# Route stage of a fused transformer kernel: two buffers for divided and residual rows, the division three trips ahead, the logits one trip later, the residual addition on GpSimd

## The reference, cut to what matters

```
ctx = einsum('bhst,bthd->bshd', attn, v).reshape(B, S, d)   # second attention, 16 heads of 16
X = X + ctx @ wo
h2 = rmsnorm(X, norm2_w).reshape(B * S, d)                  # x * rsqrt(mean(x*x) + 1e-6) * w
logits = h2 @ router_w                                      # 256 x 8
...                                                         # top 2 of 8 experts, weights
return X + moe_out                                          # and the outer: h = h + ffn(layernorm(h))
```

## Time and profile before

| | us |
|---|---|
| three runs | 825.42, 825.05, 827.81 (median 825.42) |
| the profiled execution | 832.71 |
| span of the profiled execution, first to last instruction | 830.6 |
| TensorE busy in it | 754.3 (91%) |
| VectorE busy | 465.3 (56%) |
| ScalarE busy | 376.0 (45%) |
| GpSimd busy | 189.5 (23%) |

### The profile page before, as it was taken

The page is one execution under the profiler, slowest core; times in us unless marked ns, Lnnn a source line. Parts: engine busy times, 40 slices in busy tenths (PEclk is TensorE's granted clock), DMA queues, the critical chain, the costliest instruction groups (busy, mean ns, idle before and its releaser), DMA issues. The chain is left out here.

```text
span 830.6 us, 19023 instructions
## 1 busy us (share of the span) xinstructions
PE 754.3 (91%) x7136; PEld 565.8 (68%) x7137; DVE 465.3 (56%) x1111; ACT 376.0 (45%) x616; POOL 189.5 (23%) x294
## 2 busy tenths in 40 slices
PE   4799999999988995899997888999899999999993
PEld 2366776667667884355554764555599999999992
DVE  7677666667536652799983783721244444444441
ACT  4677777777633443167764232201233333333330
POOL 5500000000003343233230220045412222222222
PEclk9999999999979999599999887999999999999997
DMA  5300000000011345344464900012423323332321
GB/s 176 146 2 2 2 3 2 2 2 2 3 46 39 102 129 168 97 125 125 115 226 144 356 1 16 0 60 79 158 63 51 47 49 45 51 50 46 45 45 19
DMA packets 70543, 58.95 MB, mean 71 GB/s; under 512 B 7552, under 2 KB 62152, under 8 KB 70480
## 3 DMA queue, kind: packets, MB, share of 16 engines
q1 hardware_dynamic: 62048, 47.61, 18.6%
q0 software_dynamic: 7152, 9.38, 6.9%
q10 hardware_dynamic: 1280, 1.08, 0.4%
HBM read 35.02 MB, written 22.95 MB: 70 GB/s over the span
## 5 line engine op out<-in xcount | busy, mean ns | idle before, releaser
L1443 POOL DMA_INDIRECT out<-ex_Y,ex_to x39 | 60.6, 1553 | 167.8 <-DVE ex_Y L1709 160.6
L1192 DVE TENSOR_REDUCE fa_m<-ps 128x2 bf16<-128x512 f32 x128 | 85.0, 685 | 8.9 <-PE ps L1063 7.3
L1162 ACT ACTIVATE fa_PT<-ps 128x1024 f32<-128x1024 f32 x64 | 65.4, 1025 | 47.7 <-PE ps L1078 45.5
L1667 DVE TENSOR_TENSOR ex_hT<-ps,ex_sl 128x512 f32<-128x512 f32 x39 | 27.0, 692 | 102.6 <-PE ps L1509 102.6
L640 ACT ACTIVATE la_PT<-ps 128x512 f32<-128x512 f32 x128 | 69.5, 594 | 25.9 <-PE ps L545 25.5
L1509 PEld LDWEIGHTS ps<-ex_xT,V 128*128 128x128 f32 x640 | 76.2, 195 | 1.7 <-ACT ex_xT L1562 0.7
L1509 PE MATMUL ps<-ex_xT,V 128*128 128x128 f32 x640 | 76.4, 279 | 0.5 <-ACT ex_xT L1562 0.5
L1516 PE MATMUL ps<-WD,ex_hT 128*128 x312 | 73.9, 380 | 0.8 <-DVE ex_Y L1709 0.8
L1509 PEld LDWEIGHTS ps<-ex_xT,XS 128*128 128x128 f32 x608 | 70.8, 192 | 1.6 <-ACT ex_xT L1562 0.7
L1509 PE MATMUL ps<-ex_xT,XS 128*128 128x128 f32 x608 | 71.1, 275 | 0.5 <-ACT ex_xT L1562 0.5
L1063 PE MATMUL ps<-QK 96*128 96x256 bf16 x256 | 53.6, 297 | 10.9 <-PEq L766 8.9
(11 more groups left out here) (260 smaller groups left out, 1430.9 us busy)
## 6 DMA issues: line engine op xcount, KB each, us to landing
QK<-qk_parts SPq DMA_DIRECT2D x192, 64.0 KB, 2.3
qk_parts<-pj_parts SPq DMA_DIRECT2D x16, 384.0 KB, 2.7
expert_in<-zfill SPq DMA_DIRECT2D x1, 5070.0 KB, 16.0
ex_XR<-expert_in SPq DMA_DIRECT2D x39, 130.0 KB, 2.1
WG<-in_e_gate SPq DMA_DIRECT2D x8, 512.0 KB, 7.8
WU<-in_e_up SPq DMA_DIRECT2D x8, 512.0 KB, 10.0
WD<-in_e_down SPq DMA_DIRECT2D x8, 512.0 KB, 9.3
out<-HS SPq DMA_DIRECT2D x4, 512.0 KB, 4.6
```

What stands on the lines that cost most here:

```text
L1162: nc.scalar.activation(PT[:, y % 2, 2 * (x % 2):2 * (x % 2) + 2], ps[:, 2 + 2 * (x % 2):4 + 2 * (x % 2)].rearrange("p k (j i) -> p k j i", ...
L1192: nc.vector.reduce_max(m[:, b % 2, grp, 2 * k:2 * k + 2], ps[:, h % 2].rearrange("p (f j) -> p f j", f=2), AX.X).then_inc(s_max, 1)
L1443: nc.gpsimd.indirect_dma_start(out=outs, out_offset=bass.IndirectOffsetOnAxis(ap=to[:, n:n + 1], axis=0), in_=Y[:, n], in_offset=None, com ...
```

## The change

- `AT` and `X2` get two buffers each, used in turn by pair.
- TensorE's trip t becomes: rows t+3, logits t-1, output t+1, divided rows t+2, normalized rows t. The last logits follow the last trip.
- VectorE's trip t becomes: X2 and moments t+1, division t+3, normalization t+1, logits copy t. Ahead of the trips stand division 0, division 1, moments 0, division 2, normalization 0.
- The addition to `HS` goes from VectorE to GpSimd, which does it as soon as X2 is there, ahead of its power (semaphore `residual`; X2 of pair i waits for the addition of pair i-2).
- ScalarE copies the turned normalized rows straight to `H2T`, from which the logits are formed; the tile `hT` and the second copy go. ScalarE now copies `ATT` of t+2 ahead of the normalized rows of t.
- The increment of `s_apart` behind bn_stats goes, and the loops of VectorE, ScalarE and GpSimd are written out.
- The banks `ps[:, 0:2]` of the rows, the bank of the output and the waits on them stay as they are.

```diff
--- before.py
+++ after.py
@@ -732,12 +732,12 @@
                             s.rec[:].unsqueeze(2).to_broadcast([P, GT * H, DK]), ALU.mult).then_inc(s.at, 1)
 
 
-def head_buffers(g, c, nc, tag):
+def head_buffers(g, c, nc, tag, n=1):
 
     def sb(n, sh):
         return c.enter_context(nc.sbuf_tensor(tag + n, sh, F32))
     s = Shared()
-    s.AT, s.ATT, s.rec = sb("AT", [P, GT, D]), sb("ATT", [P, DC, GC]), sb("rec", [P, GT * H])
+    s.AT, s.ATT, s.rec = sb("AT", [P, GT, D] if n == 1 else [P, n, GT, D]), sb("ATT", [P, DC, GC]), sb("rec", [P, GT * H])
     s.rows, s.recip, s.at, s.att, s.attc = (g.sem(tag + n) for n in ("rows", "recip", "at", "att", "attc"))
     return s
 
@@ -1204,14 +1204,15 @@
 
 
     sem, ps = g.sem, g.ps
-    (s_in, s_h, s_x2, s_var, s_r2, s_hn, s_ht, s_htc, s_h2, s_lg, s_lgk, s_dv, s_half, s_kept, s_apart) = (
-        sem("rt_" + n) for n in "in h x2 var r2 hn ht htc h2 logits lkept dve half kept apart".split())
+    (s_in, s_h, s_x2, s_var, s_r2, s_hn, s_ht, s_htc, s_lg, s_lgk, s_dv, s_half, s_kept, s_res) = (
+        sem("rt_" + n) for n in "in h x2 var r2 hn ht htc logits lkept dve half kept residual".split())
     with ExitStack() as c:
         def sb(n, sh, dt):
             return c.enter_context(nc.sbuf_tensor("rt_" + n, sh, dt))
-        s = head_buffers(g, c, nc, "rt_")
+        s = head_buffers(g, c, nc, "rt_", 2)
         st, mv, half = sb("st", [P, GT, 6], F32), sb("mv", [P, GT, 6], F32), sb("half", [P, GT], F32)
-        X2, hn, hT = sb("X2", [P, GT, D], F32), sb("hn", [P, GT, D], F32), sb("hT", [P, DC, GC], F32)
+        X2 = sb("X2", [P, 2, GT, D], F32)
+        hn = sb("hn", [P, GT, D], F32)
         w2, W, rw = sb("w2", [P, D], F32), sb("W", [P, DC, D], F32), sb("rw", [P, DC, E], F32)
         with nc.Block() as block:
             @block.sync
@@ -1228,16 +1229,27 @@
             def _(pool):
                 nc.gpsimd.memset(half[:], -0.5).then_inc(s_half, 1)
                 pool.wait_ge(s_half, 1)
-                with pool.Fori(0, GN) as t:
+                for t in range(GN):
+                    at = slice(t * GT, (t + 1) * GT)
+                    pool.wait_ge(s_x2, t + 1)
+                    nc.gpsimd.tensor_tensor(g.HS[:, at], g.HS[:, at], X2[:, t % 2], ALU.add).then_inc(s_res, 1)
                     pool.wait_ge(s_var, t + 1)
                     nc.gpsimd.tensor_tensor(mv[:, :, 4], mv[:, :, 3], half[:], ALU.pow).then_inc(s_r2, 1)
-
                     pool.wait_ge(s_hn, t * GT + GT)
-                    nc.gpsimd.tensor_copy(g.XS[:, bass.ds(t * GT, GT), 0:D], hn[:]).then_inc(s_kept, 1)
+                    nc.gpsimd.tensor_copy(g.XS[:, at, 0:D], hn[:]).then_inc(s_kept, 1)
 
             @block.tensor
             def _(pe):
                 mm = nc.tensor.matmul
+
+                def turn_att(i):
+                    pe.wait_ge(s.at, i + 1)
+                    if i:
+                        pe.wait_ge(s.attc, i)
+                    for k in range(GT):
+                        for c in range(DC):
+                            last = nc.tensor.transpose(ps[:, 2, c * GC + k * P:c * GC + (k + 1) * P], s.AT[:, i % 2, k, c * P:(c + 1) * P], g.identF[:])
+                    last.then_inc(s.att, 1)
 
                 def output(i):
                     pe.wait_ge(s.attc, i + 1)
@@ -1260,47 +1272,40 @@
                     pe.wait_ge(s_lgk, i + 1)
                     for k in range(GT):
                         for cc in range(DC):
-                            last = mm(ps[:, 5, k * E:(k + 1) * E], hT[:, cc, k * P:(k + 1) * P], rw[:, cc], start=cc == 0, stop=cc == DC - 1)
+                            last = mm(ps[:, 5, k * E:(k + 1) * E], g.H2T[:, cc, i * GC + k * P:i * GC + (k + 1) * P], rw[:, cc], start=cc == 0, stop=cc == DC - 1)
                     last.then_inc(s_lg, 1)
 
-                for i in range(2):
-                    pe_turn_rows(nc, pe, g, s, i)
-                    if i == 1:
-                        pe.wait_ge(s_in, 48)
-                        output(0)
-                    pe_turn_att(nc, pe, g, s, i)
-
-                def trip(t, ahead):
-                    if ahead:
-                        pe_turn_rows(nc, pe, g, s, t + 2)
-                    output(t + 1)
+                pe_turn_rows(nc, pe, g, s, 0)
+                pe_turn_rows(nc, pe, g, s, 1)
+                turn_att(0)
+                pe_turn_rows(nc, pe, g, s, 2)
+                pe.wait_ge(s_in, 48)
+                output(0)
+                turn_att(1)
+                for t in range(GN):
+                    if t + 3 < GN:
+                        pe_turn_rows(nc, pe, g, s, t + 3)
+                    if t:
+                        logits(t - 1)
+                    if t + 1 < GN:
+                        output(t + 1)
+                    if t + 2 < GN:
+                        turn_att(t + 2)
                     turn_normed(t)
-                    if ahead:
-                        pe_turn_att(nc, pe, g, s, t + 2)
-                    logits(t)
-
-                for t in range(GN - 2):
-                    trip(t, True)
-                trip(GN - 2, False)
-                turn_normed(GN - 1)
                 logits(GN - 1)
 
             @block.scalar
             def _(act):
                 def turned(i):
                     act.wait_ge(s_ht, i + 1)
-                    nc.scalar.activation(hT[:], ps[:, 4].rearrange("p (c t) -> p c t", c=DC), ACT.Copy).then_inc(s_htc, 1)
-                    act.wait_ge(s_htc, i + 1)
-                    nc.scalar.activation(g.H2T[:, :, bass.ds(i * GC, GC)], hT[:], ACT.Copy).then_inc(s_h2, 1)
-                    act.wait_ge(s_h2, i + 1)
-
-                for i in range(2):
-                    act_keep_att(nc, act, g, s, i, s_h)
-                with act.Fori(0, GN - 2) as t:
+                    nc.scalar.activation(g.H2T[:, :, i * GC:(i + 1) * GC], ps[:, 4].rearrange("p (c t) -> p c t", c=DC), ACT.Copy).then_inc(s_htc, 1)
+
+                act_keep_att(nc, act, g, s, 0, s_h)
+                act_keep_att(nc, act, g, s, 1, s_h)
+                for t in range(GN):
+                    if t + 2 < GN:
+                        act_keep_att(nc, act, g, s, t + 2, s_h)
                     turned(t)
-                    act_keep_att(nc, act, g, s, t + 2, s_h)
-                for i in range(GN - 2, GN):
-                    turned(i)
 
             @block.vector
             def _(dve):
@@ -1311,15 +1316,16 @@
                     dve.wait_ge(s_h, i + 1)
                     if not first(i):
                         dve.wait_ge(s_hn, i * GT)
-                    V.tensor_tensor(X2[:], ps[:, 3].rearrange("p (k d) -> p k d", d=D), g.XS[:, bass.ds(i * GT, GT), 0:D], ALU.add).then_inc(s_x2, 1)
+                    if i >= 2:
+                        dve.wait_ge(s_res, i - 1)
+                    V.tensor_tensor(X2[:, i % 2], ps[:, 3].rearrange("p (k d) -> p k d", d=D), g.XS[:, bass.ds(i * GT, GT), 0:D], ALU.add).then_inc(s_x2, 1)
                     dve.wait_ge(s_x2, i + 1)
                     for k in range(GT):
-                        do(V.bn_stats(st[:, k], X2[:, k]), s_apart)
+                        do(V.bn_stats(st[:, k], X2[:, i % 2, k]))
                         do(V.bn_aggr(mv[:, k, 0:2], st[:, k]))
                     do(V.tensor_tensor(mv[:, :, 2], mv[:, :, 0], mv[:, :, 0], ALU.mult))
                     do(V.tensor_tensor(mv[:, :, 2], mv[:, :, 2], mv[:, :, 1], ALU.add))
                     V.tensor_scalar(mv[:, :, 3], mv[:, :, 2], RMS_EPS, None, ALU.add).then_inc(s_var, 1)
-                    do(V.tensor_tensor(g.HS[:, bass.ds(i * GT, GT)], g.HS[:, bass.ds(i * GT, GT)], X2[:], ALU.add))
 
                 def rms_norm(i):
                     dve.wait_ge(s_r2, i + 1)
@@ -1327,35 +1333,41 @@
                         dve.wait_ge(s_kept, i)
                         dve.wait_ge(s_ht, i)
                     for k in range(GT):
-                        V.scalar_tensor_tensor(hn[:, k], X2[:, k], mv[:, k, 4:5], w2[:], ALU.mult, ALU.mult).then_inc(s_hn, 1)
+                        V.scalar_tensor_tensor(hn[:, k], X2[:, i % 2, k], mv[:, k, 4:5], w2[:], ALU.mult, ALU.mult).then_inc(s_hn, 1)
 
                 def keep_logits(i):
                     dve.wait_ge(s_lg, i + 1)
                     V.tensor_copy(g.LG[:, bass.ds(i * GT, GT)], ps[:, 5, 0:GT * E].rearrange("p (k e) -> p k e", e=E)).then_inc(s_lgk, 1)
 
 
+                def divide(i):
+                    dve.wait_ge(s.rows, i + 1)
+                    if i:
+                        dve.wait_ge(s.at, i)
+                    rows = ps[:, 0:GT].rearrange("p k (h d) -> p (k h) d", d=PADV)
+                    V.reciprocal(s.rec[:], rows[:, :, DK]).then_inc(s.recip, 1)
+                    dve.wait_ge(s.recip, i + 1)
+                    if i >= 2:
+                        dve.wait_ge(s.att, i - 1)
+                    V.tensor_tensor(s.AT[:, i % 2].rearrange("p k (h d) -> p (k h) d", d=DK), rows[:, :, 0:DK],
```

(26 more changed lines are left out.)

## The result

| | before | changed |
|---|---|---|
| this comparison, median (runs) | 825.23 us (4) | 844.01 us (4; 839.09 to 846.15) |
| ratio, with 95% interval | | 1.0212 [1.0163, 1.0261] |
| profiled execution / its span | 832.71 / 830.6 | 842.64 / 840.8 |
| route stage in the profile, from VectorE's first memset to the end of the last logits copy | 58.58 (445.89 to 504.47) | 71.96 (445.93 to 517.89) |

The change makes the kernel slower, by 1.6 to 2.6%, and 844.0 lies in the range given (829 to 848), 6 us above the 838. Between the two profiled executions are 10 us, because the profiled run of before was a long one among its own (832.7).

A forecast was written before the change was run, and what follows sets the result against it. VectorE's own list was taken to set the route stage's trip. Start +0.8, ring +5.3 and end -2.0 gave +4.1 us at full clock; the low clock's +8.6 made 12.7, on 825.42 thus 838 us, range 829 to 848.

The forecast's parts named there:

- the ring: Route stage: X2 of t, moments, division t+2, rows t+3, logits t-1, output t+1, X2 of t+1; 7.56 us at full clock.
- rival B: Route stage: low clock in nearly every ring and the two end rounds, +18 to +25, 843 to 850 us; chance 0.11.
- Part 1: Pairs 0 to 5: the new order of waits closes a ring, 36.99 us against 31.73, +5.3 us.
- Part 2: Start of the stage: output 0 moves behind rows 2, which wait for division 1; +0.8 us.
- Part 3: Pairs 5 to 7, no rows ahead of output 6 and 7: 18.1 us against 20.14, -2.0 us.
- Part 4: Single pieces: semaphore increments 0.22 us a pair, HS addition 1.16 on GpSimd at no cost, power 0.74.
- Part 5: TensorE in the route stage: half of the five rings at the low clock, +8.6 us.
- One for one behind the stage: Behind the route stage's barrier: a shift of the stage's end is taken one for one.
- rival C: Clock holds and first products behind the stage also run at 1.00: +1.2, 826.6 us, no change; chance 0.06.
- A: Rival: the clock holds through the route stage, +4.1, 829.5 us; chance 0.15.
- D: Rival: the ring does not bind, VectorE's list alone sets the trip, 817.5 us, faster; chance 0.08.

The follow-up runs named there:

- E7: Changed kernel with five idle TensorE products ahead of each wait of the rows for the division: 830.10 us, ratio 1.0036.
- E1: Changed kernel with VectorE's division of pair t+3 ahead of the moments of pair t+1 instead of behind them: 823.55 us, ratio 0.9957.
- E2: Changed kernel with two sets of PSUM banks for the rows, used in turn: 816.42 us, ratio 0.9877.
- E3: Changed kernel with rows t+3 behind output t+1 in TensorE's trip instead of ahead of it: 820.03 us, ratio 0.9907.
- E5: Kernel before with VectorE's division of pair t+2 behind the moments of pair t+1 instead of ahead of them: 861.95 us, ratio 1.0420.
- E6: Kernel before with only the HS addition moved to GpSimd, ahead of its power: 822.25 us, ratio 0.9929.
- E10: Changed kernel with the HS addition back on VectorE, behind the normalization: 844.36 us, ratio 1.0192.
- E8: Changed kernel unaltered, run again: 841.64 us against 827.58 for the kernel before, ratio 1.0163.

## Why the prediction was right, step by step

The mechanism was right: the ring, and the low clock that lengthens it. The closeness of the number is in part luck. In the profiles the stage grew by 13.4 us against 12.7 forecast, but from two errors that cancel: at full clock, as E7 shows it, the stage grew by 2.0 us (60.59 against 58.58) and not 4.1, and the low clock added 11.4 (71.96 against 60.59) and not 8.6. And the 18.8 us between the first medians are above the forecast's +8 to +17; 844.0 lies where rival B was to come out (843 to 850), whose condition, the low clock in nearly every ring and in the two end rounds, did not come about: the end rounds took 4.68 and 4.49 us, at a granted clock of 0.98 and 1.00.

- **The ring** (Part 1): right, in its links and its size. 7.56 worked out, 7.45 measured at full clock; pairs 0 to 5 without the clock 36.99 worked out and 36.35 measured (E7). E1, E2 and E3 each open it at another link, E5 makes it.
- **The start** (Part 2): +0.8 forecast, +0.74 measured (453.34 against 452.60).
- **The end** (Part 3): -2.0 forecast, -2.9 measured (17.23 against 20.14). The rounds took 4.68 and 4.49, not 4.84, and the last part 8.06, not 8.4. The mis-sized terms are TensorE's short pieces and VectorE's list. I took the busy time of a group (0.66 each for divided and normalized rows), but groups overlap at their ends: behind X2 of pair 5 the normalized rows start after 0.41 us (500.66 to 501.07), and E2 runs a whole trip in 4.52, where my pieces sum to 5.0. VectorE's list was given as 4.73 with a division in both rounds; behind pair 6 there is none, and that round's next X2, of pair 7, starts with no wait in front, so the 4.49 is VectorE's.
- **The pieces** (Part 4): X2 to the last moment instruction is 2.64 (453.34 to 455.98), so the semaphore increments were worth 0.25 a pair (0.22 taken); in E6, which keeps them, it is 2.87 (463.56 to 466.43). The addition takes 1.27 (1.16 taken) and leaves GpSimd 0.69 us idle ahead of the power, so it is hidden; E10 confirms that it costs and brings nothing in the ring. The power takes 0.70 (0.74 taken). That the HS addition beside it had stretched it to 1.11 is shown by E6, where the addition has left VectorE, and by E10, where it is on VectorE but elsewhere. The Trainium skill (GPSIMD Engine Reference, Key points) names contention on the shared SBUF interfaces with VectorE's instructions that have two SBUF inputs. These runs agree.
- **The clock** (Part 5): right that it is low in the ring, too small in size. I took half of five rings at the low clock, 8.6 us. It was 11.0 (47.32 less 36.35). The five rings lost 1.4, 1.7, 3.0, 3.4 and 1.5 us against those of E7, so the third and fourth were low almost throughout, as worked out for a ring at 1.2 GHz (3.5), and the others in part. The mean granted clock from X2 of pair 0 to pair 5 is 0.71, which is 58% of the time at the low level. I had argued that the pauses make the clock fall and the work lets it return; the low level fell mostly on the stretches in which TensorE works, see the last section.
- **One for one behind the stage**: not quite. The stage grew by 13.4 us in the profiles, the spans by 10.2. In the profile before, the first products behind the stage ran at 0.53 for 6 us; over the first and the fourth ten us behind the stage the granted clock was 0.69 and 0.84, in the changed kernel 0.83 and 1.00, with TensorE busy for 9.7 and 7.8 of the ten in both. At 2.4 GHz for full, that is an estimated 1.4 and up to 1.6 us, or most of the 3.2; that nothing else differs there was not tested. So the second half of rival C occurred in part, without its first: over the first six us behind the stage (518 to 524) the clock was 0.72, not 1.00. In the medians the difference is 14.1 (E8) and 18.8; why the four runs of the first comparison gave more I can't say beyond the spread of the runs, 822.4 to 833.3 for the kernel before.
- **The rivals**: A's condition, a clock that holds, is what E7 makes (830.1; 829.5 was given). D, VectorE's list alone, is what E2 makes (816.4; 817.5 was given), from the rows' banks, which the change had left single. Both times are nearer than the differences: against the kernel before of their own comparison they are +2.5 for +4.1 and -10.9 for -7.9, and that kernel's medians there were 2 us above the 825.42.

The best version is E2: 816.4 us, 1.2% below the kernel before (0.7 to 1.7%), by four runs.

## What to carry to other kernels

To run a stage further ahead, double every buffer that it passes through, here the PSUM banks of the rows and not only the SBUF tile behind them, or order the queues so that the wait is met early (E1) or that nothing which the other engine needs stands behind it (E3); otherwise the distance in trips grows while the wait stays one trip long. Before swapping two items in an in-order queue, write down the ring: the producer's item, what stands ahead of it, whom that waits for, and back; a swap is free only if each ring's sum stays below the longest engine's list. And where two engines take turns, price TensorE's part of the turn at its low clock.

## What the runs showed of the hardware that I had not expected

The clock came back in TensorE's pauses and was low for most of its work. Stretches of the changed kernel (length, TensorE busy, granted clock, DMA):

```profile
471.00:474.00 3.00, 0.24 (x3) 0.93 1.07 366
474.00:480.00 6.00, 5.90 (x22) 0.50 0.54 184
480.00:481.00 1.00, 1.00 (x6) 0.81 0.00 0
481.00:484.00 3.00, 0.73 (x7) 0.97 0.00 0
484.00:494.00 10.00, 8.79 (x32) 0.50 0.00 0
494.00:497.00 3.00, 1.60 (x15) 0.99 0.01 3
```

In these two rings the level rises about when a run of work ends, and falls about when the next begins. In the other three the run of work is partly at full clock: it falls about two microseconds into the run (at about 466.7 and 497.4) or comes back within it (at about 460). From X2 of pair 0 to that of pair 5, read in slices of 0.25 us, TensorE worked 33.4 us, 24.6 of them at the low level; of the 13.9 us in which it stood, only 2.5 were at the low level. So a stop-and-go of 2.4 to 3.1 us idle and 5 to 9 us busy paid for 1.2 GHz on three quarters of its work; spread evenly over work and pauses, the low level's 27.1 us would have held 19 of work. The pattern repeated to 0.05 us a ring in three profiles whose stages began at 445.93, 444.04 and 442.81. And filling the pause with useless products, some 2 us in each of five trips, took 11.5 us off the kernel.
